# A four-layer residual block for 32 rows, on one core: a second landing buffer for the first rows' weights, later constants, and new orders of work on every engine

## What is computed

```
x = x + x @ W[subject[b]].T + bias[subject[b]]                                   # L0, a 512x512 matrix chosen per row
x = x + layernorm(x + relu(x @ W1[lang[b]] + b1) @ W2 + b2) * gamma + beta       # L1, all chosen per row
x = x + L2(x)                                                                    # one set of weights for all rows
x = x + zX * lap_x(x) + zY * lap_y(x) + zR * x * (1 - x)                         # L3, differences along both axes
```

## Time and profile before

| | us |
|---|---|
| median of three runs | 1017.53 |
| lowest, highest | 1014.01, 1021.61 |
| the profiled execution, whole | 1015.61 |
| its span, first to last instruction | 1013.9 |
| TensorE busy | 905.2 (89%), 6088 matmuls |
| VectorE, GpSimd, ScalarE busy | 803.3, 574.8, 399.1 |
| bytes moved | 133.28 MB, mean 131 GB/s |
| mean granted TensorE clock | 0.974 |

### The profile page before, as it was taken

One profiled execution on the slowest core, in us unless ns is written; L12 is line 12 of the kernel. 1 busy time (PEld: TensorE's weight loads), 2 busy tenths in 40 slices (PEclk: granted clock), 3 DMA queues, 4 the chain that ended last, 5 costly groups with the idle time before them and its releaser, 6 DMA issues.

```text
span 1013.9 us, 18886 instructions
## 1 busy us (share of the span) xinstructions
PE 905.2 (89%) x6088; PEld 768.6 (76%) x6088; DVE 803.3 (79%) x1333; ACT 399.1 (39%) x730; POOL 574.8 (57%) x654
## 2 busy tenths in 40 slices
PE   2459999999999999999999999999999999998961
PEld 1338697888878797888979797988878797887740
DVE  4757879787987978797988979787988979786862
ACT  3464433434343442434343442534343442424220
POOL 1234627475665658475665658475665658563533
PEclk9869999999999999999999999999999999999995
DMA  6773344444434444434444444444444444421011
GB/s 225 226 240 104 104 130 131 126 138 143 136 126 145 140 142 143 139 129 153 136 126 146 142 147 145 129 137 145 135 126 146 136 143 126 127 74 32 32 42 62
DMA packets 92815, 133.28 MB, mean 131 GB/s; under 512 B 15692, under 2 KB 32588, under 8 KB 92716
## 3 DMA queue, kind: packets, MB, share of 16 engines
q1 hardware_dynamic: 88372, 125.93, 40.0%
q10 hardware_dynamic: 4344, 6.14, 1.8%
HBM read 106.86 MB, written 8.39 MB: 114 GB/s over the span
## 4 chain that ended last, share of the span: by engine, by line
DVE 32%; POOL 20%; PE 15%; issue 13%; SPq 8%; DMA 7%; ACT 4%; ACTq 1%; POOLq 0%; DVEq 0%
POOL work L417 11%; PE bank L1249 7%; DMA w_land<-in_L_cond_weight 6%; DVE w_r L831 6%; SPq L312 6%; DVE work L1009 4%; DVE work L931 3%; PE bank L1241 2%; DVE work L1016 2%; POOL work L458 2%; DVE work L1027 2%; ACT w_r L541 2%; POOL work L433 2%; PE bank L1234 2%; POOL work L447 2%
## 5 line engine op out<-in xcount | busy, mean ns | idle before, releaser
L417 POOL TENSOR_TENSOR work<-work 128x448 f32<-128x448 f32 (+3 forms) x224 | 190.9, 852 | 32.3 <-DVE work L1000 13.0
L1249 PE MATMUL bank<-x2h,wg_r 128*128 128x256 f32 x1536 | 195.9, 284 | 5.8 <-DVE bank L948 3.6
L1249 PEld LDWEIGHTS bank<-x2h,wg_r 128*128 128x128 f32 x1536 | 185.1, 189 | 17.4 <-issue 7.8
L1000 DVE TENSOR_TENSOR work<-bank,work 128x512 f32<-128x512 f32 (+7 forms) x256 | 105.7, 449 | 43.1 <-POOL work L417 21.6
L831 DVE TENSOR_TENSOR w_r<-w_land,w_r 128x1024 fp32r<-128x1024 f32 x64 | 79.0, 1235 | 45.7 <-ACT w_r L541 45.7
L1379 PE MATMUL bank<-gh,amath 128*128 128x512 f32 x384 | 105.8, 412 | 8.0 <-DVE amath L977 5.0
L433 POOL TENSOR_TENSOR work<-work 128x512 f32<-128x512 f32 x32 | 44.9, 1403 | 118.8 <-DMA work<-in_L_cond_beta 110.8
L1241 PE MATMUL bank<-w_r,xh 128*128 128x512 f32 x384 | 103.5, 414 | 9.2 <-DVE w_r L831 6.5
L1241 PE MATMUL bank<-wout_r,th 128*128 128x512 f32 x384 | 99.1, 408 | 5.2 <-DVE th L1032 3.3
L541 ACT ACTIVATE w_r<-w_land 128x1024 fp32r<-128x1024 f32 x64 | 67.7, 1057 | 87.2 <-DMA w_land<-in_L_cond_weight 80.1
L1249 PE MATMUL bank<-x2h,wsoma_r 128*128 128x256 f32 x768 | 99.4, 286 | 0.0
(11 more groups left out here) (142 smaller groups left out, 1605.1 us busy)
## 6 DMA issues: line engine op xcount, KB each, us to landing
w_land<-in_L_cond_weight SPq DMA_DIRECT2D x64, 512.0 KB, 3.8
w_t<-in_L_cond_W SPq DMA_DIRECT2D x64, 256.0 KB, 3.6
work<-work SPq DMA_DIRECT2D x64, 224.0 KB, 2.5
work<-in_xT SPq DMA_DIRECT2D x32, 256.0 KB, 3.8
b_t<-in_L_cond_bias SPq DMA_DIRECT2D x32, 256.0 KB, 4.1
work<-in_x SPq DMA_DIRECT2D x32, 256.0 KB, 3.8
gamma_t<-in_L_cond_gamma SPq DMA_DIRECT2D x32, 256.0 KB, 3.4
work<-in_L_cond_beta SPq DMA_DIRECT2D x32, 256.0 KB, 3.4
```

Source lines behind the costliest of these rows:

```text
L417: g_.tensor_tensor(dst, dst, src, ALU.add).then_inc(S["acc_ready"], 1)
L1000: ins = v_.tensor_tensor(dst, src, g_q[:, 2 * half:2 * half + 2, :, 0:width], ALU.mult)
L1249: ins = mm(dst, weight[:, w_part, first_block + a, o * P:(o + 1) * P], act[:, x_part, a], start=(not onto and a + w_part + x_part == 0), s ...
```

## The change

All computed values stay the same. What is changed:

1. **Landing buffer.** `spare_land`, 512 KB in the second half of `x2b` (which holds x2 + beta2 of odd pairs), takes half 1 of w0 for rows b = 0, 1, 2. For these rows `landing(b, half)` says where a half lands and how many splits must be over. Half 0 and half 1 have a semaphore each. The first use of that half of `x2b` (`x2_plus_beta(1, r)`) waits until six halves have been split.
2. **Constants.** `gamma2`, `beta2` leave ScalarE's queue and `zx`, `zy`, `zr` leave the head of SP's; all five are sent by `late_constants()` in step -1 of SP, behind the loads of row 0, `x` of row 1 and the first loads of pair 1. `N_CONST` becomes 7. `wn1` is sent in step -2 by ScalarE.
3. **Ids.** SP waits for subject and language numbers at their first use instead of ahead of all loads.
4. **Orders.** The lists of all five engines are new. For the middle of the run they are the old cyclic order with neighbours exchanged; at the start the preparation is placed elsewhere.

```diff
+        spare_land = buf("x2b")[:, CC // 2 * C:].rearrange("p (a c) -> p a c", a=CC // 2)
...
+        SPARE_ROWS = 3
+        def landing(b, half):
+            if b < SPARE_ROWS:
+                return (spare_land, 2 * b) if half else (w0_land[:, :, :], max(0, 2 * b - 1))
+            return w0_land[:, :, :], 2 * b - 1 if (b == SPARE_ROWS and not half) else 2 * b + half
...
-        N_CONST = 9
+        N_CONST = 7
...
-                sp.wait_ge(ids_loaded, 2 * 16)
+                def late_constants():
+                    sp.dma_start(beta2[:, :], l2_beta.partition_broadcast(P)).then_inc(beta2_loaded, 16)
+                    sp.dma_start(gamma2[:, :], l2_gamma.partition_broadcast(P)).then_inc(gamma2_loaded, 16)
+                    for dst, src in ((zraw[:, 0], zx), (zraw[:, 1], zy), (zraw[:, 2], zr)):
+                        sp.dma_start(dst, src.partition_broadcast(P)).then_inc(const2_loaded, 16)
...
+                if p == 1:
+                    pool.wait_ge(S["w0lo_ready"], 2 * SPARE_ROWS)
+                    pool.wait_ge(S["w0hi_ready"], 2 * SPARE_ROWS)
                 g_.tensor_tensor(x2b[:, p % 2, r], xs[:, r], beta2[:, :], ALU.add).then_inc(S["x2b_ready"], 1)
...
+                if not 2 * p + r:
+                    dve.wait_ge(gamma2_loaded, 16)
```

More of the change, by code:

```diff
@@ L355, in _ @@
[L355 to L357 removed]
+                        load_b0(i + 2, 1)
                 sp.wait_ge(S["out_stored"], 16 * NB)
@@ L1074, in _ @@
             for i in STEPS:
+                if live(i - 1):
+                    out_centred(i - 1, 1)
+                if i == 1:
+                    dve.wait_ge(zt_ready, 1)
+                if live(i - 1):
+                    final_sum(i - 1, 0)
+                if live(i + 1):
+                    x2_lo(i + 1, 1)
+                if live(i + 2):
+                    x1_row(i + 2, 0)
+                if live(i):
+                    temporal(i, 0)
+                if i == -1:
+                    vj_lo_parts(range(Q))
@@ new lines, in _ @@
+                if live(i - 1):
+                    final(i - 1, 0)
+                if live(i):
+                    temporal(i, 1)
+                    temporal_lo(i, 0)
+                    temporal_lo(i, 1)
+                if i == -2:
+                    decays()
+                if live(i - 1):
+                    x3_row(i - 1, 1)
+                if live(i + 2):
+                    w0_lo(i + 2, 1, 0)
+                if live(i + 1):
+                    ctx_sums(i + 1, 0)
+                if live(i):
+                    soma_gate(i, 0)
+                    soma_gate(i, 1)
@@ new lines, in _ @@
+                if live(i + 2):
+                    y_row(i + 2, 0)
+                    y_stats(i + 2, 0)
+                if live(i):
+                    soma_gate(i, 2)
+                    soma_gate(i, 3)
+                if i == -1:
+                    lo_parts(2)
+                if live(i + 2):
+                    w0_lo(i + 2, 1, 1)
+                    y_aggregate(i + 2, 0)
+                if live(i + 1):
+                    mod_split(i + 1)
+                    ctx_sums(i + 1, 1)
@@ L1075, in _ @@
+                if live(i + 2):
+                    centred(i + 2, 0)
+                if live(i - 1):
+                    final(i - 1, 1)
+                if live(i + 1):
+                    ctx_sums(i + 1, 2)
+                if live(i + 2):
+                    x2_row(i + 2, 0)
+                    x1_row(i + 2, 1)
                 if live(i + 1):
                     ctx_sums(i + 1, 3)
-                if live(i):
-                    soma_gate_lo(i, 1)
-                if live(i + 2):
-                    x2_row(i + 2, 0)
@@ L1421, in _ @@
             for i in STEPS:
+                if live(i + 1):
+                    x2_turn(i + 1, 1)
+                if live(i):
+                    state(i, 1, 3)
+                if live(i + 2):
+                    l0(i + 2, 0, BACK)
+                if live(i):
+                    spread_states(i, 1)
+                if i == -2:
+                    blend_rows()
                 if live(i):
```

461 lines of the change are left out of this document (203 added, 258 removed).

## The result

| | before | after |
|---|---|---|
| median, us | 1019.07 (1014.01 to 1021.61) | 1055.05 (1052.83 to 1056.39) |
| ratio, 95% interval | | 1.0357 [1.0311, 1.0404] |
| span of the profiled execution | 1013.9 | 1054.0 |
| mean granted clock | 0.974 | 0.971 |

The change makes the kernel 3.6% slower. I had forecast 994 and a range of 982 to 1012; the time is outside it, and on the wrong side. In short: the start gained 4 us at the end instead of 12, and the middle lost where 11 us had been expected; 31 us of the loss come back when three moves in SyncE's list are undone, of which the one of `b2` is the largest, 23 us.

What follows compares the result with a forecast made beforehand. Bounds: a row-by-row chain until 77.7 us, then TensorE, busy 55.14 us of a 57.35 us mean period. Start 12 + middle 11 = 23 us off 1015.6 gives 992.6; the median stands 1.9 higher, so 994, range 982 to 1012.

Steps and rivals of the forecast that it cites:

- the 11 us of the middle: Middle periods: reordering on VectorE and GpSimd shortens each from 57.35 to 56.52 us, 11 us over 13 periods.
- The term of the start: Start: first gates 14.7 us earlier, 2.7 given back in the first period, net 12 us, between 5 and 16.
- Constants at 8 us, half 1 split at 19.8, x1 of row 0 at 24.: Start of row 0: earlier constants and landing bring x1 from 27.17 to 24 us, -3 us (0 to -6).
- x2 of row 0 at 35, b1 of row 1 sent at 42.5, x2 of row 1 at 52.5, first gates at 63.: Start, rows 0 and 1: x2 earlier by 8 and 8.5 us, first gates 14.7 us earlier than 77.7.
- The first period gives back 2.7 us.: First period: VectorE work moved there from before 77.7 us delays gate_x(0,0) by 2 to 3 us.
- The landing buffer has little of its own.: Start: half 1 of row 0 lands by about 12.5 us instead of 20.51, but can't be used then.
- slower by two more meetings: Rival for the middle: two more POOL and VectorE meetings per period cost 2.2 us, 28 over 13 periods, 1033; chance 0.08.
- `store` behind `shift_rows`, costed at nothing.: SP, each pair: free because neighbours stands behind row_neighbours, which awaits the same shifts; otherwise up to 3.58 us per pair.
- What would show it.: Signs: first gates near 63 us, middle periods of 56.5, first period losing more than 3.7 us of TensorE time.
- the sign of being wrong: First gate after 70 us, or periods staying at 57.3 or growing, with gated, centred or soma_gate longer.
- The forecast's mechanism: Start and middle both gain, 12 and 11 us, giving 994; chance 0.55.
- The start alone: Rival: start gains 12 us, but TensorE finds other waits and periods stay at 57.3, 1005 us; chance 0.25.

Runs made afterwards that it cites:

- e8: Changed kernel with three SyncE moves undone: b2 later, next w0 and store ahead of the shifts, xT earlier; 1021.31 us, ratio 1.0049.
- e14: e1 with x_lo of the next pair ahead of x_plus_beta on GpSimd; 1021.97 us, ratio 1.0046.
- e15: e1 with rstd of the second row behind quadratic on GpSimd; 1039.81 us, ratio 1.0228.
- e2: Changed kernel with SyncE's list alone in the old order from step 0 on; 1026.8 us, ratio 1.0093.
- e1: Changed kernel's buffers, waits, constants and lists up to step -1, all engines in the old order from step 0 on; 1014.37 us, ratio 0.9961.
- e16: Kernel before with the second landing buffer and its semaphores added, lists and constants as they were; 1015.08 us, ratio 0.9989.
- e9: e1 with every half of w0 landing in one buffer again; 1029.58 us, ratio 1.0114.
- e13: e1 with x3_row of the second row ahead of w0_lo on VectorE in the middle; 1000.1 us, ratio 0.9831.
- e6: Changed kernel with half 1 of the next w0 and the store sent ahead of the first row's shifts; 1041.21 us, ratio 1.0226.
- e5: Changed kernel with b2 of the pair's first row moved back behind store and beta on SyncE; 1028.58 us, ratio 1.0131.
- e3: Changed kernel's start, compute engines in the old order from step 0 on, SyncE alone in the new order; 1273.14 us, ratio 1.2513.
- e12: Kernel before with only b2 of the first row moved early on SyncE, ahead of the second row's xT and w0; 1133.73 us, ratio 1.1129.

## Why the prediction was wrong, point by point

Two steps failed. SyncE's list was put at nothing: the move of the store with a reason that did not hold, the move of b2 without being looked at; undoing the three moves on SyncE gives 31 us back (e8). And the 11 us of the middle kept every duration fixed, where two of its three exchanges lengthen operations and cost 9 and 27 us alone (e14, e15). The term of the start was right in kind and too large, 12 for 4. The rest, some 9 to 13 us between e8 or e2 and e1, stays open.

- **Constants at 8 us, half 1 split at 19.8, x1 of row 0 at 24.** They came at 10.6, inside the bounds of 5 to 12.88. The path was as described (`exps` ends as the second split begins), each step some 2.5 us later: split at 22.3, x1 at 26.84. `l0` ran as twelve matmuls in 5.46 us and began only when both halves were split. So x1 gained 0.3 and not 3.
- **x2 of row 0 at 35, b1 of row 1 sent at 42.5, x2 of row 1 at 52.5, first gates at 63.** Measured 37.5, 44.2, 53.1 and 61.4. The step held and the gates came 16.3 us earlier, 1.6 more than I had.
- **The first period gives back 2.7 us.** This term was mis-sized. Of the 16.3 us at the first gates some 7 are the adapter and its wait, which stood between `mod` of pair 0 and the gates and now come behind them: moved and not saved. At `mod` itself the gain is 9.4. At pair 1 it is 3.0, and at the end 4 (e1). I had looked at how much room VectorE had in the earlier trace rows and not at what each piece delayed; in 52.3 us TensorE now misses 8.7 us where it missed 3.7. The net of the start was 12 in the sum, the bounds 5 to 16; e1 has 4.
- **The landing buffer has little of its own.** Right: 1 us alone (e16). What I had not seen is that the new list of loads would need it (e9).
- **The middle, 11 us from three exchanges.** `x3_row` ahead of `w0_lo` is right and larger than the whole term, -13 us (e13). `x_lo` first and `rstd` late were taken as gains and cost 9 and 27 on the old middle (e14, e15). I had subtracted their durations from the chain and kept all other durations, though the earlier trace rows showed that those depend on what runs beside them. And the short period of the earlier trace rows is not free of them: there `x_plus_b0`, at 651.78, runs beside `soma_gate`, whose two take 1.83 us for 0.73. The exchange moves a meeting, and what it costs depends on what waits behind it. The rival "slower by two more meetings" had the price of 2.2 us per period, and e15 pays 2.1, e14 0.7. It got 0.08; one of three exchanges paid it in full and one in part.
- **`store` behind `shift_rows`, costed at nothing.** This step failed, for up to 13 us. The text names the price if the cover is missing, a landing of 3.58 per pair. The cover was missing: GpSimd waits for that landing 13 times, 32.3 us in all, 4.31 us of landing are in the chain above, and e6 gets 13 us back for store and w0 together. I had argued that `neighbours` stands behind `row_neighbours`, which needs the same shifts. But the store is now sent behind those shifts and behind 512 KB of w0, so that it lands last. Store and w0 were moved back together; their shares are not separated.
- **SyncE's move of b2, not in the prediction at all.** This is the largest part, 23 us (e5). I went through the moves of waits on the computing engines and took SyncE's list as loads that come early enough. A load's place in the list has two conditions, that its data be there in time, and that its buffer be free when its turn comes. I had checked the first. The diff shows `load_b2(i + 2, 0)` ahead of xT, w0, b1, gamma, W2, a store and beta, and the code shows its wait for `x_plus_b0` of its own row, whose place on GpSimd is behind `quadratic`.
- **What would show it.** Periods grew past 57.3, as the sign of being wrong says. Its companion came only in part: `gated` got longer (498 to 614 ns), `centred` and `soma_gate` shorter (963 to 932, 981 to 627). The loss had another place.
- **The rivals.** The forecast's mechanism came in part. The kernel that has its right parts alone is e13, at 1000.1. "The start alone", 1005, would be e1, 1014. The slower side had one mechanism, the meetings, and the one that decided, SyncE's order, was not it.

## What to carry to other kernels

When a queue's order changes, go through every transfer that moved up and ask what its buffer waits for, where the operation that frees it stands on its own engine, and what it waits for; if that path leads back to a transfer that the same queue sends late, just ahead, the queue waits for itself, and all behind it waits too. Price it by what is queued behind the wait and not by the transfer: here 23 us in one order and 115 in another for the same load. And exchange neighbours one at a time: of three exchanges that all shortened the chain on paper one brought 13 us and two lost 9 and 27, and the same one had the opposite sign under other lists.

## What the runs showed of the hardware

- In e15 an operation of GpSimd on two columns, 0.19 us alone, takes 1.18 us beside VectorE's `w0_lo`, which takes 2.05 for 1.22; `x2_row` beside `quadratic` takes 1.81 for 0.73. The move of two operations of 0.8 us together was enough to bring such meetings about in every period.
- In the changed kernel the granted clock was below full mainly in the first 130 us: 0.58 in the 5 us at 101 us, in which TensorE was busy 2.06 us, and 0.74 in the 5 us behind them, in which it was busy throughout. Two periods (297.53 to 422.40) had 0.97, and the eight behind them 1.00, with 3.3 to 5.1 us of waits in each. The loss of the changed kernel is thus hardly one of clock (0.971 against 0.974 in the mean). In e3 and e12, with TensorE idle for longer stretches, the mean was 0.886 and 0.917; how much of their 255 and 115 us that makes was not separated.
